# Another order of the drain, the late table in five pieces, and the second norm's small steps moved off GpSimd

## What is computed

```python
h = concat([tokens(x, W, b, cls, pos), txt], axis=1)      # 64 x 114 x 256
h = h + attention(layernorm(h), Wq, bq, Wk, bk, Wv, bv, Wo, bo)   # linear attention, 16 heads
x = layernorm(h)
logits = x @ gate_w.T                                      # 8 experts, top 1
rw = sigmoid(max(logits)); sel = argmax(logits)
for e in range(8):
    xs = x * (rw * (sel == e))[:, None]
    out += (xs @ w_up[e].T) * silu(xs @ w_gate[e].T) @ w_down[e].T
h = h + out
```

## Time and profile before

| | |
|---|---|
| median of 3 runs | 432.34 us (431.6 to 432.51) |
| the profiled execution's own time | 431.59 us, span 429.8 us |
| PE, DVE, ACT, POOL busy | 95%, 82%, 70%, 73% of the span |
| chain that ended last | PE 83%, POOL 5%, issue 4%, DVE 3%, ACT 2% |
| GpSimd's scatters (64) and stores (64) | 75.4 us and 66.9 us busy |

### The profile page before, as it was taken

One profiled execution on the slowest core, in us unless ns is written; L12 is line 12 of the kernel. 1 busy time (PEld: TensorE's weight loads), 2 busy tenths in 40 slices (PEclk: granted clock), 3 DMA queues, 4 the chain that ended last, 5 costly groups with the idle time before them and its releaser, 6 DMA issues.

```text
span 429.8 us, 13564 instructions
## 1 busy us (share of the span) xinstructions
PE 406.6 (95%) x4389; PEld 399.4 (93%) x4389; DVE 352.1 (82%) x1140; ACT 298.8 (70%) x760; POOL 312.0 (73%) x699
## 2 busy tenths in 40 slices
PE   8999999999999999999999999999988999999940
PEld 7999899999999999999999999999887999999940
DVE  5678568999999999999999999998796887777840
ACT  5444477688778778878877877886684777777720
POOL 4065213688888888888888888888867777777772
PEclk9999999999999999999999999999998999999995
DMA  8965111333322231331121112100683589422220
GB/s 299 353 207 165 51 48 47 99 98 87 111 90 64 64 100 39 92 116 44 38 64 51 39 54 60 54 25 24 182 229 104 183 243 283 164 86 88 75 92 14
DMA packets 34152, 46.49 MB, mean 108 GB/s; under 512 B 8843, under 2 KB 25857, under 8 KB 34083
## 3 DMA queue, kind: packets, MB, share of 16 engines
q1 hardware_dynamic: 24860, 30.50, 23.5%
q0 software_dynamic: 9216, 15.12, 11.2%
q10 hardware_dynamic: 6, 0.00, 0.0%
HBM read 26.87 MB, written 17.17 MB: 102 GB/s over the span
## 4 chain that ended last, share of the span: by engine, by line
PE 83%; POOL 5%; issue 4%; DVE 3%; ACT 2%; DMA 1%; POOLq 0%; SPq 0%; DVEq 0%; ACTq 0%
PE b_kg L1491 8%; PE b_kg L1492 8%; PE b_kg L1493 8%; PE b_w L1491 8%; PE b_w L1492 7%; PE b_w L1493 7%; PE b_att L1606 6%; PE b_t L1556 3%; PE b_v L1493 3%; PE b_v L1491 3%; PE b_v L1492 3%; PE b_t L1620 3%; PE b_att L1543 3%; PE b_att L1491 3%; PE b_att L1493 2%
## 5 line engine op out<-in xcount | busy, mean ns | idle before, releaser
L705 POOL DMA_INDIRECT sorted_rows<-rows,place x64 | 75.4, 1177 | 20.3 <-issue 9.4
L831 POOL DMA_INDIRECT out<-result,rows_all x64 | 66.9, 1045 | 19.5 <-issue 12.8
L937 ACT ACTIVATE q_exp<-b_w,bq_s 128x228 f32<-128x228 f32 x64 | 28.9, 451 | 24.0 <-PE b_w L1493 23.9
L1491 PE MATMUL b_w<-xnT_hi,wq_hi 128*128 128x264 f32 x128 | 39.6, 309 | 0.2
L1491 PE MATMUL b_kg<-wkgv_hi,xnT_hi 128*114 128x264 f32 x128 | 38.7, 302 | 0.4 <-DVE patch_out L1128 0.4
L1040 ACT ACTIVATE silu_g<-b_kg,rows_all 128x128 f32<-128x128 f32 x64 | 23.5, 368 | 21.8 <-PE b_kg L1493 19.6
L1491 PE MATMUL b_kg<-wgu_hi,xsT_hi 128*128 x128 | 37.2, 290 | 0.0
L1492 PE MATMUL b_w<-xnT_lo,wq_hi 128*128 128x264 f32 x128 | 36.5, 285 | 0.0
L1492 PE MATMUL b_kg<-wkgv_lo,xnT_hi 128*114 128x264 f32 x128 | 36.5, 285 | 0.0
L1492 PE MATMUL b_kg<-wgu_lo,xsT_hi 128*128 x128 | 36.4, 285 | 0.0
L1493 PE MATMUL b_kg<-wkgv_hi,xnT_lo 128*114 128x264 f32 x128 | 36.4, 284 | 0.0
(11 more groups left out here) (252 smaller groups left out, 1647.4 us busy)
## 6 DMA issues: line engine op xcount, KB each, us to landing
rows_all<-sorted_rows SPq DMA_DIRECT2D x64, 130.0 KB, 3.3
rows_all<-in_x SPq DMA_DIRECT2D x18, 384.0 KB, 4.3
rows_all<-in_txt SPq DMA_DIRECT2D x32, 154.0 KB
rows_all<-in_wgu_in SPq DMA_DIRECT2D x8, 256.0 KB, 3.0
rows_all<-patch_out SPq DMA_DIRECT2D x48, 36.0 KB
sorted_rows<-tail_rows SPq DMA_DIRECT2D x9, 130.0 KB
sorted_rows<-rows,place POOLq DMA_INDIRECT x64, 3.7
rows_all<-in_wdown_in SPq DMA_DIRECT2D x2, 512.0 KB, 4.2
```

Of the source, the lines that this page charges most:

```text
L705: G.indirect_dma_start(out=scratch[0:EXPERTS * REGION, :], out_offset=bass.IndirectOffsetOnAxis(ap=place[:, k, b:b + 1], axis=0), in_=rows ...
L831: G.indirect_dma_start(out=out, out_offset=bass.IndirectOffsetOnAxis(ap=rows_all[:, t.n, ID:ID + 1].bitcast(I32), axis=0), in_=result[:, k ...
L937: S.activation(q_exp[:, c, :], at, ACT.Exp, bias=bq_s[:, c:c + 1])
L1491: T.matmul(to, left_hi, right_hi, start=start, stop=False, skip_group_check=seeded)
```

## The change

- `rstd2_of` keeps three instructions (variance plus epsilon, times 4; the power; `ratio`), which gives half of 1/deviation. The statistics go straight into the row's fields. ScalarE makes the negated mean (`means`) and the gain (`gains`, two instructions: half times tanh plus half).
- `places` is one product and one dependent reduce that writes integers, in place of two fused product-and-sums and their accumulator reads. The ids are copied ahead of the scatter (`ids_in`). `scatter` is the two DMAs alone; it waits for gain, centring, place and id.
- In the step, GpSimd counts right behind the scatter; `early_rows` is called at the head of step 30 and not at the end of step 29, which is the same place in its queue.
- The drain has another order on all four engines; stores of twos 0, 1 and 2 stand between the last scatters, the last of which follows six stores. `stats_2(31)`, `centred(31)` and the last tanh come after some duo_steps.
- The late table on VectorE is `late_ends`, `late_past`, `late_sums`, `late_rows` behind duo_steps 4, 5, 6, 7, with `late_count` behind 3.

```diff
             def rstd2_of(p):
                 pool.wait_ge(mv2_ready, p + 1)
                 if p >= 1:
-                    pool.wait_ge(rstd2_step, 5 * p)
-                if p >= 1:
+                    pool.wait_ge(rstd2_step, 3 * p)
                     pool.wait_ge(top_n_ready, p)
                 if p >= 4:
-                    pool.wait_ge(centred_ready, p - 3)
-                G.tensor_scalar(ve2[:], mv2[:, k, :, 1], LN_EPS, None, ALU.add).then_inc(rstd2_step, 1)
-                G.tensor_scalar(mean_neg[:, k, :], mv2[:, k, :, 0], -1.0, None, ALU.mult).then_inc(rstd2_step, 1)
-                pool.wait_ge(rstd2_step, 5 * p + 1)
-                G.tensor_tensor(rstd2[:, k, :], ve2[:], half_neg[0:TOK, :], ALU.pow).then_inc(rstd2_step, 1)
-                pool.wait_ge(rstd2_step, 5 * p + 3)
-                G.tensor_copy(rows[:, k, :, MEAN], mv2[:, k, :, 0]).then_inc(rstd2_step, 1)
+                    pool.wait_ge(gain_ready, p - 3)
+                G.tensor_scalar(ve2[:], rows[:, k, :, GAIN], LN_EPS, 4.0, ALU.add, ALU.mult).then_inc(rstd2_step, 1)
+                pool.wait_ge(rstd2_step, 3 * p + 1)
+                G.tensor_tensor(rstd2_half[:, k, :], ve2[:], half_neg[0:TOK, :], ALU.pow).then_inc(rstd2_step, 1)
+                pool.wait_ge(rstd2_step, 3 * p + 2)
                 pool.wait_ge(rstd1_step, 5 * p + 5)
...
+            def ids_in(p):
+                if p >= 4:
+                    pool.wait_ge(scattered[p % 4], 32 * (p // 4))
+                G.tensor_copy(rows[:, p % 4, :, ID].bitcast(I32), ids_s[:, 2 * p:2 * p + 2]).then_inc(id_ready, 1)
             def scatter(p):
-                pool.wait_ge(tanh_ready, p + 1)
+                pool.wait_ge(gain_ready, p + 1)
                 pool.wait_ge(centred_ready, p + 1)
-                G.tensor_scalar(route_w[:], tanh_top[:, p % 2, :], 1.0, 0.5, ALU.add, ALU.mult).then_inc(field_step, 1)
-                G.tensor_copy(rows[:, k, :, ID].bitcast(I32), ids_s[:, 2 * p:2 * p + 2]).then_inc(field_step, 1)
-                pool.wait_ge(field_step, 4 * p + 1)
-                G.tensor_tensor(rows[:, k, :, GAIN], route_w[:], rstd2[:, k, :], ALU.mult).then_inc(field_step, 1)
                 pool.wait_ge(place_ready, p + 1)
-                G.tensor_copy(place[:, k, :], place_f[:, k, :]).then_inc(field_step, 1)
-                pool.wait_ge(field_step, 4 * p + 4)
+                pool.wait_ge(id_ready, p + 1)
...
             count_chosen(PAIRS - 2)
             scatter(PAIRS - 3)
             rstd2_of(PAIRS - 2)
+            ids_in(PAIRS - 2)
             top_value(PAIRS - 2)
+            store(Turn(0, 0))
+            count_chosen(PAIRS - 1)
             scatter(PAIRS - 2)
-            count_chosen(PAIRS - 1)
+            store(Turn(0, 1))
             rstd2_of(PAIRS - 1)
+            ids_in(PAIRS - 1)
             top_value(PAIRS - 1)
+            store(Turn(0, 2))
             scatter(PAIRS - 1)
+            for m in range(3, DUOS):
+                store(Turn(0, m))
...
+            def gains(p):
+                act.wait_ge(tanh_ready, p + 1)
+                for b in range(2):
+                    half = rstd2_half[:, p % 4, b:b + 1]
+                    last = S.activation(rows[:, p % 4, b, GAIN:GAIN + 1], tanh_top[:, p % 2, b:b + 1], ACT.Identity, bias=half, scale=half)
+                last.then_inc(gain_ready, 1)
+            def means(p):
+                act.wait_ge(mv2_ready, p + 1)
+                if p >= 1:
+                    act.wait_ge(centred_ready, p)
+                S.activation(mean_neg[:], rows[:, p % 4, :, MEAN], ACT.Copy, scale=-1.0).then_inc(mean_neg_ready, 1)
...
                     tanh(i - 4)
+                if 0 <= i - 3:
+                    means(i - 3)
                 if 0 <= i:
                     keys(i)
+                if 0 <= i - 4:
+                    gains(i - 4)
...
             attention_high(PAIRS - 1)
+            tanh(PAIRS - 3)
             gate_and_up(Turn(0, 0))
+            gains(PAIRS - 3)
             rows_high(Turn(0, 2))
-            tanh(PAIRS - 3)
             act_high(Turn(0, 0))
             gate_and_up(Turn(0, 1))
+            means(PAIRS - 2)
+            centred(PAIRS - 2)
             rows_high(Turn(0, 3))
-            centred(PAIRS - 2)
             tanh(PAIRS - 2)
             act_high(Turn(0, 1))
             gate_and_up(Turn(0, 2))
+            gains(PAIRS - 2)
             rows_high(Turn(0, 4))
+            gate_and_up(Turn(0, 3))
+            act_high(Turn(0, 2))
+            rows_high(Turn(0, 5))
+            duo_step(Turn(0, 4))
+            duo_step(Turn(0, 5))
+            means(PAIRS - 1)
             centred(PAIRS - 1)
+            duo_step(Turn(0, 6))
             tanh(PAIRS - 1)
-            straight(STEPS_B, duo_step)
+            gains(PAIRS - 1)
+            straight(range(7, DUOS + 1), duo_step)
...
-                for b in range(2):
-                    last = V.tensor_tensor_reduce(place_e[:, b, :], rank_bank(p)[:, b * EXPERTS:(b + 1) * EXPERTS],
-                                                  chosen[:, p % 2, b, :], 1.0, 0.0, ALU.mult, ALU.add,
-                                                  place_f[:, p % 4, b:b + 1])
-                last.then_inc(place_ready, 1)
+                V.tensor_tensor(place_e[:], rank_bank(p).rearrange("p (b e) -> p b e", b=2), chosen[:, p % 2], ALU.mult).then_inc(place_step, 1)
+                dve.wait_ge(place_step, p + 1)
+                with nc.allow_low_precision(reason="one whole number and zeros are summed"):
+                    V.tensor_reduce(place[:, p % 4, :], place_e[:], AX_X, ALU.add).then_inc(place_ready, 1)
...
             rows_low(Turn(0, 1))
+            places(PAIRS - 3)
             attention_low(PAIRS - 1)
             act_of(Turn(0, 0))
-            places(PAIRS - 3)
...
             result_of(Turn(0, 0))
+            places(PAIRS - 2)
+            rows_low(Turn(0, 3))
+            act_low(Turn(0, 1))
             route(PAIRS - 1)
-            rows_low(Turn(0, 3))
-            places(PAIRS - 2)
-            stats_2(PAIRS - 1)
-            act_low(Turn(0, 1))
...
             duo_step(Turn(0, 4))
-            late_slots()
+            late_ends()
+            stats_2(PAIRS - 1)
             duo_step(Turn(0, 5))
+            late_past()
+            duo_step(Turn(0, 6))
+            late_sums()
+            duo_step(Turn(0, 7))
             late_rows()
-            straight(range(6, DUOS + 2), duo_step)
+            straight(range(8, DUOS + 2), duo_step)
...
             gate_up(Turn(0, 2), 1).then_inc(gu_done, 1)
+            turn_rows(Turn(0, 4))
             down(Turn(0, 1))
+            first_products(Turn(0, 3))
+            gate_up(Turn(0, 3), 0).then_inc(gu_done, 1)
             rank(PAIRS - 1)
-            turn_rows(Turn(0, 4))
-            duo_step(Turn(0, 3))
+            gate_up(Turn(0, 3), 1).then_inc(gu_done, 1)
+            turn_act(Turn(0, 2))
+            turn_rows(Turn(0, 5))
             late_count()
```

More of the change, by code:

```diff
@@ L221, in build @@
             stats2 = sb("stats2", [TOK, 2, 6], at=room)
-            mv2 = sb("mv2", [TOK, 4, 2, 2], at=room)
             ve2 = sb("ve2", [TOK, 2], at=room)
-            rstd2 = sb("rstd2", [TOK, 4, 2], at=room)
-            mean_neg = sb("mean_neg", [TOK, 4, 2], at=room)
+            rstd2_half = sb("rstd2_half", [TOK, 4, 2], at=room)
+            mean_neg = sb("mean_neg", [TOK, 2], at=room)
             ratio = sb("ratio", [TOK, 2], at=room)
@@ L438, in build @@
         EXPERT_LOAD = 16
-        STEPS_B = range(3, DUOS + 1)
         GU_STEPS, DOWN_STEPS = (8, 9, 11, 12, 14, 15, 17, 18), (20, 21)
@@ L814, in _, with store @@
                 step(i)
+            def store(m):
+                for t in tiles_of(m):
+                    k = t.slot(RESULT_RING)
+                    pool.wait_ge(result_ready, t.n + 1)
+                    G.indirect_dma_start(
+                        out=out, out_offset=bass.IndirectOffsetOnAxis(ap=rows_all[:, t.n, ID:ID + 1].bitcast(I32), axis=0),
+                        in_=result[:, k, :], in_offset=None,
+                        bounds_check=TOKENS - 1, oob_is_err=False).then_inc(stored[k], 16)
             count_chosen(PAIRS - 2)
@@ L817, in _ @@
             rstd2_of(PAIRS - 2)
+            ids_in(PAIRS - 2)
             top_value(PAIRS - 2)
+            store(Turn(0, 0))
+            count_chosen(PAIRS - 1)
             scatter(PAIRS - 2)
-            count_chosen(PAIRS - 1)
+            store(Turn(0, 1))
             rstd2_of(PAIRS - 1)
+            ids_in(PAIRS - 1)
             top_value(PAIRS - 1)
+            store(Turn(0, 2))
             scatter(PAIRS - 1)
-            def duo_step(j):
-                if (j - 1).within(DUOS):
-                    m = j - 1
-                    for t in tiles_of(m):
-                        k = t.slot(RESULT_RING)
-                        pool.wait_ge(result_ready, t.n + 1)
-                        G.indirect_dma_start(
```

(22 more changed lines are left out.)

30 lines of the change are left out of this document (16 added, 14 removed).

## The result

The changed kernel takes 0.9929 of the time of the one before, 95% interval 0.9907 to 0.9952: 428.67 us (median, 428.05 to 429.9) against 432.31. A second measurement on another chip gave 0.9930 (0.9917 to 0.9943). By the ratio that is 3.1 us, where 2.0 were forecast. The range holds by a hair: the forecast for the median was 430.3, its lower bound 428.6, and the median 428.67 lies 0.07 above that bound. The ratio, put on the 432.34 of before, gives 429.3.

A forecast was written before the change was run, and what follows sets the result against it. TensorE was taken to bound the steady stretch, tied with a loop through VectorE and ScalarE, and GpSimd's stores the end. Step 30's -0.9 and the drain's -1.1 made -2.0: median 430.3 us, range 428.6 to 432.6.

The forecast's parts named there:

- Step 30: Rank's hole at step 30: mean_neg moved from GpSimd to ScalarE no longer delays centring; -0.9 us, bounds 0 and -1.0.
- the "nothing" of the steady stretch: Steady steps: relieving GpSimd gains nothing, since nobody in the loop waits for it; the longer places costs nothing either.
- ScalarE and places: Steady step: ScalarE's three added instructions (0.4 us) covered by its wait before den; places 0.30 within 0.36 room.
- Rival D: Steady loop: places over 0.36 us delays attnT_lo, every 0.01 paid by 26 steps; 432.6 at 0.45; chance 0.10.
- TensorE in the drain: Drain: +0.25 later start, -1.85 hole before down(1), -1.7 half clock avoided, -0.1 hitch; -3.4 to -3.7 us.
- the shift: The earlier arrival of everything after step 30, forecast at 0.9 us and left out of GpSimd's drain times.
- rival C: Drain: TensorE's clock falls anyway, three microseconds at half clock costing it 1.9 us; 431.9 to 432.9; chance 0.10.
- the lock: Drain: stores starting inside act_u are held, fixing GpSimd's lag behind results; 3.65 us before, forecast 6.41.
- the addition at the end: After TensorE's last work: GpSimd's stores are two places further behind, paid as 2 x 1.27 = +2.55 us.
- Rival A: Drain: store(3) 0.4 us later puts the lag at 7.69, one store further behind; +1.27, 431.6; chance 0.15.
- rival B: Drain: GpSimd slips one or two stores closer (429.0 or 427.8), or never locks (-1.5, 428.8); chance 0.14.
- Late table, late loads: Drain: VectorE's spread table work costs nothing, at worst 0.3 us; loads starting 1 us later covered by 10 us.

The follow-up runs named there:

- fill: Changed kernel with store(2) moved ahead of rstd2(31), into GpSimd's wait, and store(3) ahead of the last scatter; 0.9894 of the kernel before, 427.52 us.
- one_operand: Changed kernel with act_of's product of two SBUF operands replaced by a reduce of up_g alone (different result); 0.9857 of the kernel before, 424.92 us.
- drain_only: Kernel before with only the new drain order, spread late table and later last scatter, old small steps kept; 1.0005 of the kernel before, 431.10 us.
- places_pad: Changed kernel with two unused products added on VectorE ahead of the one in places; 0.9985 of the kernel before, 430.39 us.
- the pads: Changed kernel with five or ten small GpSimd copies between scatter(31) and store(3); 0.9961 (430.42 us) and 0.9914 (428.37 us) of the kernel before.
- psum_up2: Changed kernel with VectorE multiplying up from PSUM by gain and silu, ScalarE's copy dropped, waits split by tile; 0.9881 of the kernel before, 426.99 us.
- after_again: Changed kernel unaltered, measured again on another chip; 0.9930 of the kernel before, 429.22 us.
- pad_hole: Changed kernel with seven unused bn_stats on VectorE ahead of act_low(1), delaying down(1); 1.0030 of the kernel before, 433.21 us.
- after: The changed kernel itself, as first measured; 0.9929 of the kernel before, 428.67 us.
- psum_fill: Kernel of psum_up2 with store(2) and store(3) ahead of the last pair's small steps and scatter; 0.9863 of the kernel before, 425.85 us.
- norm_only: Changed kernel's new small steps, route and places with the old drain order, late table and stores; 0.9971 of the kernel before, 430.00 us.

## Why the prediction held, point by point

**What bounds it.** Right: TensorE in the steady stretch (50.00 of 50), GpSimd at the end. fill, one_operand and drain_only each show that TensorE's gain and the end are two things.

**Step 30.** Right in kind: its period went from 9.23 to 8.22, ScalarE's wait of 1.85 is gone, -1.0. But the first column fell by 1.50. The step that failed is the "nothing" of the steady stretch: I had read the 8.59 step of the earlier trace rows as a price for VectorE's lateness and not asked whether its cause, a pause put down to issue (0.27 at 248.44), would survive a change in the number of VectorE's instructions. The steps of 8.37 and 8.60 became 8.25 (0.47 us less), against one new step of 8.33 (ScalarE, 0.22 before den at 117.6).

**ScalarE and places.** Hidden, as forecast. 0.55 a step instead of 0.4 on ScalarE; 0.28 for places (0.30 forecast), so the spare is there, and places_pad with 0.16 more is past it. Rival D's price was too high: 0.1 past the edge, places_pad pays 0.02 a step in the even stretch (8.27 on the mean against 8.25), not its full lateness.

**TensorE in the drain.** -3.85 against -3.4 to -3.7. Down(1) starts at 325.50, as worked out (326.8 without the shift), with no hole at all (0.2 forecast); turn_act(0) is 0.11 later than the shift alone, not 0.25. The clock held, and was worth the 1.7 reckoned: the lower clock cost that in all three kernels that have the hole. So hole and clock are 2.05 and 1.71 of the 3.85. The 1.26 us hole before the last apply stayed and again left the clock up, so rival C's condition didn't arise.

**GpSimd.** The wait was 2.08 (2.3 forecast), store(3) 7.31 behind (7.0 to 7.2), the lock 6.38 to 6.43 (6.41), the addition at the end +2.55 (+2.55). Rival A is real, 0.4 us away: drain_only starts at 8.36 and goes there. Of rival B, the late table's work let nothing slip here; that a lock can be lost, and that there can be none, the pads and one_operand show. What failed is the price of no lock. I had -1.5 for no lock at all. From store(3) at 342.55, 57 stores at 1.27 lead to 415, which one_operand shows (415.21): -4. My own 0.23 a two, over 28 twos, made some 6 us of catching up; the 1.5 was a slip that I didn't hold against it. So I took the lock for a small matter, though it costs 3.1 us by the ratios and 4.05 by the sums, as much as the whole change brought (3.1 and 2.81) or more.

**Late table, late loads.** Nothing in the rows: TensorE has no wait over 0.26 us between down(1) and the end.

**The chances.** One sum in them is off: the rest of A, C and half of D are 0.25 and not 0.21, and slower is then 0.05.

## What to carry to other kernels

Where one queue ends last and is behind by a whole number of its own items, work out its lag at the start of the loop and the places where it can come to rest: gains ahead of that loop then count in steps (here 1.28 us) for as long as the lock holds, and five small instructions can be worth more than their length. It need not hold: the pads lost it to 0.03 us. Look for a periodic 0.97, 1.20 in a row of equal DMA issues and for the instruction of the neighbouring engine that ends when the long one is released; giving that instruction one operand from PSUM took the last column from 10.26 to 6.08 here, of which 2.1 us were left in the whole by the ratios (0.9881 against 0.9929). Cut spans at events that all versions share before comparing them.

## What the runs showed of the hardware

- An indirect store on GpSimd that begins 0.05 to 0.26 us into a VectorE tensor_tensor with two SBUF operands is held until that ends (1.02 to 1.23 instead of 0.97, 187 times); one that begins 0.04 into it goes first and the VectorE instruction takes 0.50 instead of 0.43 (4 times). With one SBUF operand (reduce), with PSUM and one SBUF operand (tensor_tensor), or with PSUM, a scalar column and one SBUF operand there was no holding: in psum_up2 every store of the twos from 4 on took 0.97 or 0.98. The Trainium skill (SBUF — State Buffer, Who interferes with whom) says that who issues first gets the shared pair for the whole instruction, while the other is blocked. These rows agree that either engine can be the one that waits. They don't show it for the whole instruction: VectorE lost 0.07 us to a store of 0.98. The section's inference that a tensor_tensor leaves descriptor generation alone doesn't hold for these indirect stores. It also says that a VectorE instruction with two SBUF inputs contends with a GpSimd instruction that reads SBUF. An indirect store takes its row ids from SBUF, so that this rule would fit; no run here tells the two readings apart.
- VectorE paused for 0.20 and 0.27 us after its 524th and 708th recorded instruction in three kernels, wherever these fell, and not there in kernels with 64 instructions fewer. Other such pauses were 0.24 after the 150th in after_again and pad_hole, and not in after, which is the kernel of after_again; and 0.29 after the 988th in psum_fill. The Trainium skill (Runtime: NRT & Kernel Launch, Instruction fetch mechanics) has an engine's instructions come in blocks, with the crossing mostly hidden. Whether these pauses are such crossings, no run here shows.
- 2.05 to 2.20 us of idle time on TensorE, in the drain, were followed by the lower of the two clock levels for 3.4 us, 1.7 us lost, in three orders of work (before, norm_only, pad_hole). Idle times of 0.8 to 1.35 us were not, in any of the profiles, and neither was one of 1.99 us that psum_fill has at its start (7.37 to 9.37).
